# Moving parts of TensorE's float32r operands by 64 bytes within SBUF: x, routed and shared weights of a residual expert block

## The reference, cut to what matters

```python
x = x + L0(x)   # per sequence: a mix of 8 masked 128x128 matrices, and a bias
x = x + L1(x)   # per sequence: a base matrix and 8 low-rank updates, weighted by cond_8
x = x + L2(x)   # shared expert and the top-2 of 8 routed experts: down(gelu(x@gate) * (x@up)), inner size 512
x = x + L3(x)   # the top-1 of 8 experts: down(silu(x@up + b) * (x@gate + b)) + b, inner size 256
```

## Time and profile before

| | before |
|---|---|
| median of 3 runs | 134.24 us (134.16 to 134.31) |
| the profiled execution | 134.94 us |
| its span (first to last instruction) | 133.1 us |
| TensorE matmul busy | 128.1 us, 930 records |
| weight loads busy | 119.5 us |
| VectorE, ScalarE, GpSimd busy | 99.2, 99.1, 75.2 us |

### The profile page before, as it was taken

One profiled execution on the slowest core, in us unless ns is written; L12 is line 12 of the kernel. 1 busy time (PEld: TensorE's weight loads), 2 busy tenths in 40 slices (PEclk: granted clock), 3 DMA queues, 4 the chain that ended last, 5 costly groups with the idle time before them and its releaser, 6 DMA issues.

```text
span 133.1 us, 3284 instructions
## 1 busy us (share of the span) xinstructions
PE 128.1 (96%) x930; PEld 119.5 (90%) x930; DVE 99.2 (75%) x193; ACT 99.1 (74%) x205; POOL 75.2 (57%) x89
## 2 busy tenths in 40 slices
PE   7799999999999999999999999999999999999990
PEld 5688888888888899999999999999999999999980
DVE  0499898797775867758868677677777676898791
ACT  3774699979956487777887877866767669989860
POOL 0038539979990028368497685963542644426770
PEclk9999999999999999999999999999999999999999
DMA  4999999999104955657766567656577565664224
GB/s 135 295 396 413 407 400 404 400 397 400 64 0 176 375 212 223 246 225 288 290 255 244 231 250 315 267 229 246 222 304 305 220 258 224 270 284 188 79 86 158
DMA packets 11490, 34.56 MB, mean 260 GB/s; under 512 B 1104, under 2 KB 2512, under 8 KB 11472
## 3 DMA queue, kind: packets, MB, share of 16 engines
q1 hardware_dynamic: 11184, 34.15, 65.7%
q10 hardware_dynamic: 288, 0.20, 0.5%
HBM read 12.32 MB, written 1.05 MB: 100 GB/s over the span
## 4 chain that ended last, share of the span: by engine, by line
PE 85%; DMA 3%; DVE 3%; ACT 1%; POOL 1%; issue 1%; SPq 1%; ACTq 0%; DVEq 0%; POOLq 0%
PE gate L298 29%; PE up L298 29%; PE acc L298 28%; DMA slabs<-third_in 3%; DVE x_res L978 1%; DVE h_pair L906 1%; DVE up L987 1%; POOL x_lo L762 1%; POOL x_res L788 1%; ACT h_pair L619 0%; ACTq L224 0%; ACT h_act L672 0%; DVE h_pair L1010 0%; SPq L258 0%; DVE acc L1003 0%
## 5 line engine op out<-in xcount | busy, mean ns | idle before, releaser
L756 POOL TENSOR_TENSOR dn_lo<-slabs,dn_hi 128x256 fp32r<-128x256 f32 x40 | 29.7, 743 | 38.9 <-ACT dn_hi L637 38.8
L613 ACT ACTIVATE h_act<-gate 128x512 f32<-128x512 f32 x48 | 28.9, 602 | 23.1 <-PE gate L298 21.1
L906 DVE TENSOR_TENSOR h_pair<-up,h_pair 128x512 fp32r<-128x512 f32 x55 | 37.6, 683 | 0.0
L916 DVE SCALAR_TENSOR_TENSOR up<-h_act,w_route,up 128x512 f32<-128x512 f32 x32 | 24.2, 755 | 16.9 <-PE up L298 16.7
L298 PE MATMUL gate<-x_hi,w_gu 128*128 128x256 f32 x160 | 33.9, 276 | 0.0
L298 PE MATMUL up<-x_hi,w_gu 128*128 128x256 f32 x158 | 33.4, 276 | 0.0
L619 ACT ACTIVATE h_pair<-up 128x512 fp32r<-128x512 f32 x55 | 32.8, 597 | 0.0
L298 PEld LDWEIGHTS gate<-x_hi,w_gu 128*128 128x128 f32 x160 | 27.1, 188 | 0.2
L298 PEld LDWEIGHTS up<-x_hi,w_gu 128*128 128x128 f32 x158 | 26.8, 188 | 0.0
L298 PE MATMUL acc<-h_pair,dn_hi 128*128 128x256 f32 x140 | 25.5, 276 | 0.0
L298 PE MATMUL gate<-x_lo,w_gu 128*128 128x256 f32 x80 | 22.1, 276 | 0.0
(11 more groups left out here) (126 smaller groups left out, 200.0 us busy)
## 6 DMA issues: line engine op xcount, KB each, us to landing
w_gu<-slabs SPq DMA_DIRECT2D x40, 512.0 KB, 3.1
slabs<-slabs_moe SPq DMA_DIRECT2D x8, 768.0 KB, 13.1
slabs<-slabs_l SPq DMA_DIRECT2D x4, 768.0 KB, 9.0
sh_raw<-slabs_shared SPq DMA_DIRECT2D x2, 384.0 KB, 5.8
x_res<-x_rest SPq DMA_DIRECT2D x1, 768.0 KB, 7.5
outT<-x_res SPq DMA_DIRECT2D x6, 128.0 KB, 2.0
slabs<-second_in SPq DMA_DIRECT2D x1, 320.0 KB, 3.1
slabs<-third_in SPq DMA_DIRECT2D x1, 256.0 KB, 4.6
```

Of the source, the lines that this page charges most:

```text
L613: nc.scalar.activation(h_act[:, u % 2, :], gate_ps[u % 2][:], ACT.Gelu_apprx_tanh).then_inc(act_done, 1)
L756: nc.gpsimd.tensor_tensor(dn_lo[:, q % W_SLOTS, :], slab_cols(at, DOWN_AT, 256), dn_hi[:, q % W_SLOTS, :].bitcast(F32), ALU.subtract).then ...
L906: V.tensor_tensor(h_lo[:, u % H_SLOTS, :], h_of(u), h_hi[:, u % H_SLOTS, :].bitcast(F32), ALU.subtract).then_inc(h_lo_done, 1)
L916: ins = V.scalar_tensor_tensor(h_of(u), h_act[:, k, :], weight, h_of(u), ALU.mult, ALU.mult)
```

## The change

`x_hi` and `x_lo` become 128 columns longer and are read through one slice for each pair; the slices of a pair begin 0 or more columns of 4 bytes late. The same is done with the slots of `w_gu` (high and low part apart) and with the second half of `sh_lo`. `sh_hi`, `dn_hi`, `dn_lo` and `h_pair` are only accessed in another notation. `place_sh` is allocated earlier, so that small tiles in between move by some bytes.

```diff
-        x_hi = sb("x_hi", [P, TOKENS], F32R)
-        x_lo = sb("x_lo", [P, TOKENS], F32R)
+        x_hi_all, x_lo_all = (sb(n, [P, TOKENS + 128], F32R) for n in ("x_hi", "x_lo"))
+        x_hi = [x_hi_all[:, p * PAIR + at:(p + 1) * PAIR + at] for p, at in enumerate((0, 0, 16, 16))]
+        x_lo = [x_lo_all[:, p * PAIR + at:(p + 1) * PAIR + at] for p, at in enumerate((0, 16, 32, 48))]
+        place_sh = sb("place_sh", [P, 24])
...
-        place_sh = sb("place_sh", [P, 24])
         sh_hi = sb("sh_hi", [P, HALVES * SLAB], F32R)
-        sh_lo = sb("sh_lo", [P, HALVES * SLAB], F32R)
+        sh_lo_all = sb("sh_lo", [P, HALVES * SLAB + 128], F32R)
+        sh_lo_half = [sh_lo_all[:, k * (SLAB + 16):k * (SLAB + 16) + SLAB] for k in range(HALVES)]
         place_w = sb("place_w", [P, 16])
-        w_gu = sb("w_gu", [P, W_SLOTS, 2 * SLAB_GU], F32R)
+        w_gu_all = sb("w_gu", [P, W_SLOTS * 2 * SLAB_GU + 128], F32R)
+        w_gu = [[w_gu_all[:, at + (2 * k + part) * SLAB_GU:at + (2 * k + part + 1) * SLAB_GU]
+                 for part, at in enumerate(places)] for k, places in enumerate(((0, 0), (0, 16), (16, 32), (48, 48)))]
+        w_dma = [w_gu_all[:, 2 * k * SLAB_GU + at:2 * k * SLAB_GU + at + 2 * (SLAB_GU + gap)].rearrange(
+            "p (a w) -> p a w", a=2)[:, :, 0:SLAB_GU] for k, (at, gap) in enumerate(((0, 0), (0, 16), (16, 16), (48, 0)))]
...
-                sp.dma_start(w_gu[:, q % W_SLOTS, :].bitcast(F32),
-                             slab_cols(at, 0, 2 * SLAB_GU)).then_inc(d_gu[q % W_SLOTS], DMA)
+                sp.dma_start(w_dma[q % W_SLOTS].bitcast(F32),
+                             slab_cols(at, 0, 2 * SLAB_GU).rearrange("p (a w) -> p a w", a=2)).then_inc(d_gu[q % W_SLOTS], DMA)
...
-                    split_product(out[:], sh_hi[:, w], sh_lo[:, w], x_hi[:, tok], x_lo[:, tok]).then_inc(done, 1)
+                    split_product(out[:], sh_hi[:, w], sh_lo_of(w), x_of(x_hi, tok), x_of(x_lo, tok)).then_inc(done, 1)
...
-                return (w_gu[:, slot, off:off + P], w_gu[:, slot, SLAB_GU + off:SLAB_GU + off + P])
+                return tuple(part[:, off:off + P] for part in w_gu[slot])
```

More of the change, by code:

```diff
@@ L156, in build @@
         place_h = sb("place_h", [P, 112])
-        h_pair = sb("h_pair", [P, H_SLOTS, 2, 512], F32R)
-        h_hi, h_lo = h_pair[:, :, 0, :], h_pair[:, :, 1, :]
+        h_all = sb("h_pair", [P, H_SLOTS, 2, 512], F32R)
+        h_pair = [h_all[:, k, :, :] for k in range(H_SLOTS)]
+        h_hi, h_lo = [h[:, 0, :] for h in h_pair], [h[:, 1, :] for h in h_pair]
         out_part = sb("out_part", [P, 2, S])
@@ L225, in slab_of, with sh_lo_of, x_of @@
                                      max_val=(SLABS_EXPERTS + SLABS_L3 - 1) * WIDE)
+        def sh_lo_of(cols):
+            k = cols.start // SLAB
+            return sh_lo_half[k][:, cols.start - k * SLAB:cols.stop - k * SLAB]
+        def x_of(parts, tok):
+            p = tok.start // PAIR
+            return parts[p][:, tok.start - p * PAIR:tok.stop - p * PAIR]
         def slab_cols(at, offset, n):
@@ L407, in shared_up @@
                 at = (c // 2) * SLAB + (c % 2) * P
-                tok = bass.ds(p * PAIR, PAIR)
+                tok = slice(p * PAIR, (p + 1) * PAIR)
                 for out, off, done in ((gate_ps[c % 2], 0, gate_ready), (up_ps[c], 256, up_ready)):
                     w = slice(at + off, at + off + P)
-                    split_product(out[:], sh_hi[:, w], sh_lo[:, w], x_hi[:, tok], x_lo[:, tok]).then_inc(done, 1)
+                    split_product(out[:], sh_hi[:, w], sh_lo_of(w), x_of(x_hi, tok), x_of(x_lo, tok)).then_inc(done, 1)
             def first_shared_up():
@@ L418, in first_shared_up @@
                 for out, w, _ in parts:
-                    mm(out[:], sh_hi[:, w], x_hi[:, 0:PAIR], True, False)
+                    mm(out[:], sh_hi[:, w], x_hi[0][:], True, False)
                 pe.wait_ge(sh_lo_ready, 1)
                 for out, w, _ in parts:
-                    mm(out[:], sh_lo[:, w], x_hi[:, 0:PAIR], False, False)
+                    mm(out[:], sh_lo_of(w), x_hi[0][:], False, False)
                 pe.wait_ge(x2_lo, 1)
                 for out, w, done in parts:
-                    mm(out[:], sh_hi[:, w], x_lo[:, 0:PAIR], False, True).then_inc(done, 1)
+                    mm(out[:], sh_hi[:, w], x_lo[0][:], False, True).then_inc(done, 1)
             def hidden_split(u):
@@ L446, in shared_down @@
                 w = slice(at, at + P)
-                split_product(acc(p, 512), sh_hi[:, w], sh_lo[:, w], h_hi[:, c, :], h_lo[:, c, :],
+                split_product(acc(p, 512), sh_hi[:, w], sh_lo_of(w), h_hi[c][:, :], h_lo[c][:, :],
                               c == 0, c == 3).then_inc(down_done, 1)
@@ L467, in slab_up @@
                         w_hi, w_lo = gate_up_split(q, off + c * P)
-                        last = split_product(out[:, c * S:(c + 1) * S], w_hi, w_lo, x_hi[:, tok], x_lo[:, tok])
+                        last = split_product(out[:, c * S:(c + 1) * S], w_hi, w_lo, x_of(x_hi, tok), x_of(x_lo, tok))
                     last.then_inc(done, 1)
@@ L478, in slab_down @@
                     last = split_product(out, dn_hi[:, q % W_SLOTS, w], dn_lo[:, q % W_SLOTS, w],
-                                         h_hi[:, u % H_SLOTS, h], h_lo[:, u % H_SLOTS, h],
+                                         h_hi[u % H_SLOTS][:, h], h_lo[u % H_SLOTS][:, h],
                                          start and c == 0, stop and c == 1)
@@ L545, in last_gate_up @@
                         w_hi, w_lo = gate_up_split(q, off + c * P)
-                        split_product(out, w_hi, w_lo, x_hi[:, tok], x_lo[:, tok]).then_inc(done, 1)
+                        split_product(out, w_hi, w_lo, x_of(x_hi, tok), x_of(x_lo, tok)).then_inc(done, 1)
             def last_down():
@@ L557, in last_down @@
                     last = split_product(l3_acc(t), dn_hi[:, t % 4, w], dn_lo[:, t % 4, w],
-                                         h_hi[:, t % 4, h], h_lo[:, t % 4, h], c == 0, c == 1)
+                                         h_hi[t % 4][:, h], h_lo[t % 4][:, h], c == 0, c == 1)
                 last.then_inc(down_done, 1)
@@ L595, in round_x2 @@
                 for b in (2 * p, 2 * p + 1):
-                    last = nc.scalar.activation(x_hi[:, b * S:(b + 1) * S], x2_ps(b), ACT.Identity, bias=c_b[:, b:b + 1])
+                    last = nc.scalar.activation(x_of(x_hi, slice(b * S, (b + 1) * S)), x2_ps(b), ACT.Identity, bias=c_b[:, b:b + 1])
                 last.then_inc(x2_hi, 1)
@@ L605, in _ @@
             act.wait_ge(acc_read, ACC_BIAS)
-            nc.scalar.activation(x_hi[:, 0:S], x2_ps(0), ACT.Identity, bias=c_b[:, 0:1]).then_inc(x2_hi_half, 1)
+            nc.scalar.activation(x_hi[0][:, 0:S], x2_ps(0), ACT.Identity, bias=c_b[:, 0:1]).then_inc(x2_hi_half, 1)
             round_shared(1)
@@ L618, in round_h @@
                     act.wait_ge(down_done, u + 1 - H_SLOTS)
-                nc.scalar.activation(h_hi[:, u % H_SLOTS, :], h_of(u), ACT.Copy).then_inc(h_hi_done, 1)
+                nc.scalar.activation(h_hi[u % H_SLOTS][:, :], h_of(u), ACT.Copy).then_inc(h_hi_done, 1)
             def round_expert(e):
@@ L691, in _ @@
                 h = slice(c * S, (c + 1) * S)
-                nc.scalar.activation(h_hi[:, t % 4, h], last_up[c], ACT.Copy).then_inc(h_hi_done, 1)
+                nc.scalar.activation(h_hi[t % 4][:, h], last_up[c], ACT.Copy).then_inc(h_hi_done, 1)
             add_bias(4)
@@ L716, in lo_shared @@
                 pool.wait_ge(sh_hi_ready, k + 1)
-                nc.gpsimd.tensor_tensor(sh_lo[:, at], sh_raw[:, at],
+                nc.gpsimd.tensor_tensor(sh_lo_half[k], sh_raw[:, at],
                                         sh_hi[:, at].bitcast(F32), ALU.subtract).then_inc(sh_lo_ready, 1)
@@ L761, in lo_x3 @@
                 at = slice(b * S, (b + 1) * S)
-                nc.gpsimd.tensor_tensor(x_lo[:, at], x_res[:, at], x_hi[:, at].bitcast(F32),
+                nc.gpsimd.tensor_tensor(x_of(x_lo, at), x_res[:, at], x_of(x_hi, at).bitcast(F32),
                                         ALU.subtract).then_inc(x3_lo, 1)
@@ L878, in _ @@
             dve.wait_ge(x2_first_sum, 2)
-            V.tensor_scalar(x_hi[:, S:2 * S], x2_ps(1), c_b[:, 1:2], None, ALU.add).then_inc(x2_hi, 1)
+            V.tensor_scalar(x_hi[0][:, S:], x2_ps(1), c_b[:, 1:2], None, ALU.add).then_inc(x2_hi, 1)
             def split_x2(p):
@@ L885, in split_x2 @@
                     at = slice(b * S, (b + 1) * S)
-                    last = V.scalar_tensor_tensor(x_lo[:, at], x2_ps(b), c_b[:, b:b + 1], x_hi[:, at].bitcast(F32),
+                    last = V.scalar_tensor_tensor(x_of(x_lo, at), x2_ps(b), c_b[:, b:b + 1], x_of(x_hi, at).bitcast(F32),
                                                   ALU.add, ALU.subtract)
@@ L905, in lo_h @@
                 dve.wait_ge(h_hi_done, u + 1)
-                V.tensor_tensor(h_lo[:, u % H_SLOTS, :], h_of(u),
```

(7 more changed lines are left out.)

## The result

The changed kernel takes 137.25 us (137.10 to 137.59) against 134.24 us: ratio 1.021, 95% interval 1.018 to 1.024. It is slower, as forecast, but by 3.0 us where 1.3 were forecast, and outside the range, which ended at 137.0.

What follows compares the result with a forecast made beforehand. TensorE's matmul pitch was taken to bound the kernel. Copies and other engines' writes at 0, plus 0.94 and 0.37 us of slower matmuls, together 1.3 us, gave a median of 135.5 us, range 133.1 to 137.0.

Steps and rivals of the forecast that it cites:

- What bounds the kernel, and the other engines: TensorE, 96% busy at full clock, sets the time by its matmuls' pitch; VectorE, ScalarE and GpSimd writes add 0.
- The copies: Copies to `w_gu`, half now with two runs a partition, land 3.1 us after issue, due after 6.8: 0 added.
- Two pitches for one matmul: On TensorE the same matmul takes 113.3 or about 118 ns at 256 columns, 226.7 or about 233 at 512.
- (3): TensorE's own reads: matmuls with changed remainders take the slow pitch, together 1.3 us more; chance 0.32.
- the 224 and the 56: Gate and up matmuls now at like remainders, 0.94 us; shared-unit matmuls now at unlike remainders, 0.37 us.
- They follow on changed ones: Routed and L3 down products keep their remainders but come after changed matmuls; no price was given.
- Everything unsettled: TensorE stays in the slow pitch throughout, down products too: 3.6 us more, 137.8 us; chance 0.10.
- No effect: Changed remainders leave each of TensorE's 771 matmuls its pitch: 134.2 us; chance 0.32.
- Faster: Some new placements free TensorE's float32r matmuls of their price over float32: 1.1 us gained, 133.1 us; chance 0.25.
- Copies late: TensorE waits about 1 us for copies to `w_gu` in each of 20 units, 20 us; chance 0.01.
- What would show it: Signs in the stretch of 540 matmuls: mean pitch 114 to 115.5 ns, unlike between units, no TensorE wait for `w_gu`.

Runs made afterwards that it cites:

- the controls: Changed kernel with every shift 0 (ratio 1.000), with shifts of multiples of 256 bytes (1.000) or 512 bytes (1.002); kernel before with everything 64 bytes further (1.002).

## Why the prediction was right in direction and wrong in size

**What bounds the kernel, and the other engines: right.** TensorE's pitch is the time, the clock stayed full, and the controls put layout, copies and writes at nothing.

**The copies: right.** Landing stayed at 3.1 us. Only the issue, 644 ns for two runs and 512 for one where it was 494, wasn't foreseen; it is hidden.

**Two pitches for one matmul: right, and shown.** The extra matmuls switch between them at a distance of 64.

**The step that failed is (3), the count: "I price the 224 and the 56 at the slow pitch".** Behind the shared part, gate and up were priced at 0.94 us and cost 1.9; routed down products were priced at nothing and cost 0.63. It was mis-sized in three ways.

It took the remainder by 128, where a modulus of 256 matters. By 256 only 148 of the 480 gate and up matmuls keep the distance of 64 (132 stand at 0, 92 at 128, 108 at 192), and three units of forty keep it throughout. So 332 changed, not 224.

It took a different distance as a thing that unsettles, at 4.2 ns. Uniform kernels without any change of distance stand 6.7 ns over the quick pitch at 0 and 128, and 4.5 at 192. An estimate from these, 224 x 6.7 + 108 x 4.5 ns = 2.0 us, already stands above the whole forecast. It is rough, and that it comes near the measured 1.9 is in part luck: units at 0 and 128 only (96.11 us in the chain) took 118.0 ns and not 120.0, and unchanged gate and up matmuls were slow too.

And it left matmuls of unchanged distance at the quick pitch. Most don't have it: the changed kernel's down products kept their operands' remainders, and their rows take 0.68 to 0.71; the unit at 53.74 us kept all its distances and has 117.8 ns. "They follow on changed ones" stood in the prediction, without a price. That `sh_lo` alone, 24 matmuls, costs 2.6% is the plainest case. The shared part, +0.45 us, was forecast at 0.37.

**The rivals.** "Everything unsettled", 137.8 us at a chance of 0.10, is closest: 137.25. For it I had the right row, twelve slow matmuls with nothing changing among them, and should have seen that a kept pitch makes the share of changed matmuls the wrong measure. It is not wholly right, since the unit at 112.95 us and some down products settle within the mixture. Its sum was miscounted: routed and L3 units have 40 x 18 = 720 matmuls of 256 columns, not 627, which makes 4.0 us and 138.2. (The 6.6 ns at 512 columns are 233.3 - 226.7, not 233 - 226.7.) "No effect" falls. Its rule in the Trainium skill (SBUF — State Buffer, Who interferes with whom), by which TensorE's two read ports are independent and it never waits on anyone, was that rival's ground, and its forecast of no change fails: at distances 0 and 64 the same program has 120.0 and 113.3 ns. Whether the two ports wait for each other no run shows. "Faster" fell too: no distance tried gave less than 113.3 or 226.7 ns. That 226.7 ns is a fixed price of float32r was argued there and stays unshown. "Copies late" falls.

**What would show it.** I wrote 114 to 115.5 ns, and it was 117.5. Units are unlike, as written, between 116 and 119 ns. Of the two places named as worst, pair 0 with slot 3 is the slowest unit of the stretch (0.72 and 0.72 at 60.10 us); pair 3 with slot 0 isn't (0.71 and 0.71 at 96.11 us); by 256 its distances are 0 and 128.

**What stays open.** Why 256 and 512 columns have different quick distances; why 64 and 192 have two pitches each, and what decides in which one TensorE ends (which matmuls, waits or shapes); and the mechanism. That the running weight load and the streaming operand meet in the same part of SBUF fits a price that hangs on their distance by 256 bytes, but no run separates it from other causes, nor tells the matmul's own weights from those loaded beside it.

## What to carry to other kernels

Where TensorE is the bound, its pitch is worth more than its busy share: divide a long stretch by its matmuls, and where one shape shows two pitches, look at what stands around both. Such a pitch can hang on the placement of the weights against the streaming operand and be kept over hundreds of matmuls, so a change to 24 of them can cost as much as one to all. Sweep the distance in uniform steps, one shape at a time, before varying it by part, and don't take the pitch of one uniform kernel for the price of its distance (192 bytes had two); and when pricing such an edit, count what comes behind it, not only what it touches.

## What the runs showed of the hardware

- float32r matmuls of 256 columns, each with a weight load of 128 columns, at full clock: 113.3 ns at a distance of 64 bytes, 117.3 to 120.0 ns at 0, 32, 96, 128 and 192, in kernels where all routed operands keep that distance. At 192 single units had 113.3 ns in the kernel with doubled shifts. The pattern repeats after 256 bytes (shifts by 256 and 512 changed nothing, by 128 they did), and moving all operands together by 64 changes nothing.
- The same with 512 columns: 226.7 ns at distance 0 and 233.3 ns at 64 in long stretches; at 0 three at a time between routed units took 233 ns each.
- At 64 bytes and 256 columns the pitch of 117.8 ns stayed from the third routed unit to the end with `sh_lo` alone shifted, and three matmuls of 512 columns put in between brought 113.3 ns, to the last whole unit. At distances 0 and 192 they changed nothing that lasted.
- Copies of 512 KB within SBUF: 644 ns to issue with two runs a partition, 512 with one in the same kernel, 494 in the kernel before; landing 3.1 us in both kernels.
